# Two-layer kernel on one Trainium2 core: ranks counted with shifted keys, SSM step sizes of the first batch from TensorE, first tiles copied within SBUF, last outputs begun in two parts, and a new order of layer 1

## The reference, cut to what matters

```python
# L1_attn: a Mamba block; d_inner 512, 16 states
xz = x @ W_in.T; u, z = split(xz)
u = silu(causal_conv4(u) + b); dt, Bm, Cm = split(u @ W_x.T)      # dt: one value per token
delta = softplus(dt * W_dt + b_dt)                                # 512 channels
h_t = exp(delta_t * A) * h_(t-1) + delta_t * u_t * B_t            # 512 channels x 16 states
y = (sum_n h * C + D * u) * silu(z) @ W_out.T
# L1_ffn: light attention in windows of 128 (8 heads), plus heavy attention of 256 routed queries
scores = coor_descent(x . routing_token, k)                       # 50 iterations
sel = top_k(scores, 256)                                          # equal scores: the earlier token first
```

## Time and profile before

| what | value |
|---|---|
| three runs | 1880.72, 1887.73, 1896.94 us; median 1887.73 |
| the profiled execution | 1893.86 us, its span 1892.1 us |
| mean granted TensorE clock | 0.959 of full speed |
| busy over the span | PE 89%, DVE 81%, POOL 72%, ACT 71% |
| layer 1 starts | 633.2 us |
| first scan, end of the last product with C | 699.8 us, 1875.4 us |
| batch 0: end of du 0.0, scan 2, end of `ranks`, scan 18 | 678.5, 703.9, 731.8, 749.5 us |

### The profile page before, as it was taken

One profiled execution on the slowest core, in us unless ns is written; L12 is line 12 of the kernel. 1 busy time (PEld: TensorE's weight loads), 2 busy tenths in 40 slices (PEclk: granted clock), 3 DMA queues, 4 the chain that ended last, 5 costly groups with the idle time before them and its releaser, 6 DMA issues. The chain is left out here.

```text
span 1892.1 us, 44180 instructions
## 1 busy us (share of the span) xinstructions
PE 1687.4 (89%) x13508; PEld 1025.8 (54%) x13508; DVE 1540.8 (81%) x2806; ACT 1337.3 (71%) x3257; POOL 1354.6 (72%) x1115
## 2 busy tenths in 40 slices
PE   6899899799697568879999999989999999999987
PEld 4576576576475234335556546545545645644645
DVE  6547657556437789999999999999989999999997
ACT  4566566465364486776887896897797798787775
POOL 2706615806806228879899899889889889988996
PEclk9899899799798889989999999999999999999999
DMA  9346345445436563435236435346436346454430
GB/s 293 100 130 139 109 125 125 138 141 128 119 101 160 163 179 105 132 122 143 81 127 168 119 94 168 101 114 168 123 114 167 102 130 159 105 143 133 118 89 24
DMA packets 160088, 245.77 MB, mean 130 GB/s; under 512 B 30672, under 2 KB 105040, under 8 KB 159856
## 3 DMA queue, kind: packets, MB, share of 16 engines
q1 hardware_dynamic: 147568, 226.15, 42.3%
q0 software_dynamic: 12288, 16.79, 4.3%
HBM read 169.39 MB, written 73.47 MB: 128 GB/s over the span
## 5 line engine op out<-in xcount | busy, mean ns | idle before, releaser
L2254 POOL TENSOR_TENSOR HB<-DD,BC 128x512 f32<-128x512 f32 x512 | 643.4, 1285 | 110.5 <-DMA DD<-dd_scratch 55.1
L2581 ACT ACTIVATE bank<-DD,A 128x512 f32<-128x512 f32 x512 | 349.9, 696 | 138.1 <-DVE HB L2792 89.1
L2260 POOL TENSOR_TENSOR HB<-HB,BC 128x512 f32<-128x512 f32 x256 | 323.5, 1279 | 61.1 <-DVE HB L2787 58.4
L2787 DVE TENSOR_TENSOR_SCAN bank<-bank,HB 128x512 f32<-128x512 f32 x256 | 310.7, 1214 | 16.6 <-ACT bank L2581 15.1
L2787 DVE TENSOR_TENSOR_SCAN HB<-bank,HB 128x512 f32<-128x512 f32 x256 | 310.0, 1211 | 17.0 <-ACT bank L2581 14.5
L2792 DVE TENSOR_TENSOR HB<-bank,BC 128x512 f32<-128x512 f32 x256 | 174.8, 683 | 14.5 <-DVE bank L2787 0.5
L692 POOL DMA_INDIRECT X<-expert_out_scratch,slot x64 | 112.2, 1752 | 67.3 <-DMA expert_out_scratch<-YS 39.5
L2303 PE MATMUL bank<-HB,fold 128*32 128x512 f32 x1024 | 138.6, 613 | 22.9 <-DVE HB L2792 9.5
L2393 PE MATMUL bank<-ident,PR 128*128 128x128 f32 x768 | 115.3, 283 | 27.6 <-ACT PR L2619 18.8
L2303 PE MATMUL bank<-XRT,Wk 128*128 128x512 f32 x256 | 126.0, 625 | 11.2 <-ACT Qa L2595 8.6
L2393 PEld LDWEIGHTS bank<-ident,PR 128*128 128x128 f32 x768 | 86.5, 143 | 89.0 <-issue 40.0
(11 more groups left out here) (289 smaller groups left out, 3756.8 us busy)
## 6 DMA issues: line engine op xcount, KB each, us to landing
DD<-dd_scratch SPq DMA_DIRECT2D x512, 128.0 KB, 3.4
ROW<-row_scratch SPq DMA_DIRECT2D x64, 256.0 KB
BC<-ssm_scratch SPq DMA_DIRECT2D x128, 128.0 KB, 4.2
US<-us_scratch SPq DMA_DIRECT2D x32, 512.0 KB, 4.6
XL<-sorted_scratch SPq DMA_DIRECT2D x92, 128.0 KB, 2.1
expert_out_scratch<-YS SPq DMA_DIRECT2D x92, 128.0 KB, 1.8
us_scratch<-U SPq DMA_DIRECT2D x8, 1024.0 KB, 5.5
us_scratch<-SD SPq DMA_DIRECT2D x7, 1024.0 KB, 7.6
```

Of the source, the lines that this page charges most:

```text
L2254: done(pool.tensor_tensor(HB[:, c % HR], du, bc, ALU.mult), "dbu")
L2260: done(pool.tensor_tensor(h, h, bc, ALU.mult), "cg")
L2581: done(act.activation(PD[n % 2][:], delta, ACT.Exp, scale=A[:, k:k + 1]), "dA")
L2787: done(dve.tensor_tensor_scan(h if n % 2 else dA, dA, h, 0.0, ALU.mult, ALU.add), "scan")
```

## The change

1. **Ties.** `before` and L2774 go. The keys are also stored to a scratch `keypad` (a row of 256 per tile: 128 entries of -1, then the tile's 128 keys). A new step `w_ld` of each batch reads for partition p the 128 values that end just before token p's own key: KW, in the second half of Sel. The ties are then the count of equal values, a `tensor_scalar` with accumulation on KW alone. `ranks` becomes one `tensor_reduce` over 128 x 4 x 3. `w_ld` waits on SP for `del` b.1 (and the earlier readers of Sel), and each `rank` waits on DVE for the window to land. The first half of `keypad` is filled by one DMA from a memset.
2. **dt of batch 0.** A new step `dtb` on PE: four matmuls with column 0 of W_x broadcast to 128 columns put dt on all partitions of a bank; `abs` and `relu` of batch 0 read it there. `dt_ld` 0 goes. `ssm` 0 stays, for B and C, and stands behind `dtb` on PE.
3. **First tiles.** DD tiles 0 to 5 of batch 0 no longer come from `dd_scratch`: SP copies them from SD and U in SBUF, 8 DMAs of 32 x 512 per tile, after `del` 0.0 and `du` 0.0. `dd_st` of batch 0 is one step for all 512 channels; it waits for `del`, `du` 0.1 and for these copies to have landed.
4. **Tables.** The table with exp and ln is loaded just ahead of the first step that needs it after a silu. `gsilu` 0 moves up behind `silu`.
5. **Last outputs.** In batch 7, `tail` is split: `tailp` does the selection part and gates 0 to 2 of a tile's output, `tail` only the last matmul.
6. **Order.** All of `L1_ORDER` is written anew.

The diff, cut to its core (the order table is left out):

```diff
-    return [(kind, b, i)] if kind in ("in", "xt", "st") or kind in COPIES.values() else []
+    if kind == "tailp" or (kind == "tail" and b == B - 1):
+        return [("tail", b, i)] if kind == "tailp" else []
+    return [(kind, b, i)] if kind in ("in", "xt", "st", "dtb") or kind in COPIES.values() else []
...
+        KW = KJ[:, 1].rearrange("p (t j) -> p t j", t=NT)
...
+                def w_ld(b):
+                    sp.wait_ge(over["key_out"], 48)
+                    sp.wait_ge(over["pad_out"], 16)
+                    after(sp, "del", b, 1)
+                    after(sp, "xg", b - 1, 0)
+                    after(sp, "st", b - 1, 0, 1)
+                    earlier = scr["keypad"][b * NT:(b + 1) * NT]
+                    window = bass.AP(earlier.tensor, earlier.offset, [[1, P], [2 * P, NT], [1, P]])
+                    sp.dma_start(KW, window).then_inc(over["window_in"], 16)
...
-                def first_dd_st():
+                def first_dd_ld(i):
+                    after(sp, "del", 0, 0)
                     after(sp, "du", 0, 0)
-                    for c, src in enumerate((SD, U)):
-                        sp.dma_start(scr["dd"][0, 0:2 * P, c].rearrange("(k p) t -> p k t", p=P), src[:, pair(0)]) \
-                          .then_inc(over["first_dma"], 16)
+                    k, rows = i // 4, slice(32 * (i % 4), 32 * (i % 4) + 32)
+                    for st in range(4):
+                        for c, src in enumerate((SD, U)):
+                            sp.dma_start(DD[32 * st:32 * st + 32, i, c], src[rows, k]).then_inc(over[f"dd_in{i}"], 16)
...
                 def dd_st(b):
+                    after(sp, "del", b, 0, 1)
                     after(sp, "du", b, 0, 1)
+                    if b == 0:
+                        for i in range(DDS):
+                            sp.wait_ge(over[f"dd_in{i}"], 128)
...
+                def first_steps():
+                    loaded(pe, 0, "small_in")
+                    bank = claimed(pe, "dtb", 0, 0)
+                    for k in range(NB):
+                        after(pe, "silu", 0, k)
+                        q = mm(bank[:], Wx[:, k, 0:1].broadcast_to([P, P]), U[:, k], k == 0, k == NB - 1)
+                    done(q, "dtb")
...
+                for what, b, i in plan:
+                    if what in SILUS1:
+                        with_exp = False
+                    elif what in EXPS1 and not with_exp:
+                        load_ln_exp(act)
+                        with_exp = True
...
                 def rank(b, t):
...
                     dve.wait_ge(over["key_in"], 32 * (b + 1))
+                    dve.wait_ge(over["window_in"], 16 * (b + 1))
...
-                    own(dve.scalar_tensor_tensor(out=KJ[:, 1, 0:P], in0=KR[:, own_tile], scalar=KC[:, t:t + 1],
-                                                 in1=before[:], op0=ALU.is_equal, op1=ALU.mult,
-                                                 accum_out=ties[:, t:t + 1]))
+                    own(dve.tensor_scalar(KW[:, t], KW[:, t], KC[:, t:t + 1], None, ALU.is_equal, ALU.add,
+                                          accum_out=ahead[:, t, 2:3]))
...
-                    own.now(dve.tensor_tensor(ties[:], ties[:], ahead[:, 1], ALU.add))
-                    done(dve.tensor_tensor(ties[:], ties[:], ahead[:, 0], ALU.add), "ranks")
+                    done(dve.tensor_reduce(ties[:], ahead[:], X_AXIS, ALU.add), "ranks")
```

More of the change, by code:

```diff
@@ new lines @@
+    "gsilu": [[73]],
+    "us_st": [[76, 184], [506], [1129], [1818], [2368], [3113], [3660], [4312]],
+    "dtb": [[77]],
+    "abs": [[78, 79, 81, 82], [605, 571, 572, 607], [1181, 1170, 1171, 1182], [1852, 1819, 1820, 1853], [2439, 2431,
+        2438, 2455], [3117, 3115, 3116, 3122], [3776, 3722, 3723, 3777], [4372, 4371, 4380, 4373]],
+    "sexp": [[80, 102], [635], [1205], [1868], [2498], [3139], [3791], [4409]],
+    "ssm": [[87], [531], [1136], [1766], [2392], [3041], [3683], [4305]],
+    "ssmc": [[88], [532], [1137], [1767], [2393], [3042], [3692], [4309]],
@@ L1897, in pairs_of @@
     return sorted({m // 2 for m in items_of(a)})
+SILUS1, EXPS1 = {"silu", "gsilu"}, {"es", "asc", "sexp", "sln", "dA", "expl", "exp"}
 COPIES = {"xrtc": "xrt", "zc": "z", "ssmc": "ssm", "projc": "proj", "xgc": "xg", "turnc": "turn", "tailc": "tail", "spreadc": "spread"}
@@ L1922, in bank_freed @@
         return "pv", b, i if kind == "widenc" else NT + i
+    if kind == "relu" and b == 0:
+        return ("dtb", 0, 0) if i == NB - 1 else None
     if kind in HALVES:
@@ L2192, in _ @@
                         k_ld(b)
+                    elif what == "w_ld":
+                        w_ld(b)
                     elif what == "x_ld":
@@ L2238, in constants @@
                     own(pool.memset(half[:], -0.5))
[L2239 to L2243 removed]
+                    own(pool.memset(pad, -1.0))
+                    own.now(pool.memset(fold[:], 0.0))
                     for r in range(4):
@@ L2443, in fold_states, with tail_begun @@
                     done(q, "fold")
-                def tail(b, t):
-                    after(pe, "gate", b, *range(NB))
+                def tail_begun(b, t):
                     after(pe, "widenr", b, 0, 1)
@@ L2463, in _ @@
                         scan_in(what, b, i)
+                    elif what == "dtb":
+                        first_steps()
                     elif what == "ssm":
@@ L2483, in _ @@
                         fold_states(b, i)
+                    elif what == "tailp":
+                        tail_begun(b, i)
                     elif what == "tail":
@@ L2623, in widened_reciprocals @@
                     after(act, "rec", b, a)
+                    if b == 0 and a == 0:
+                        act.wait_ge(over["pad_out"], 16)
                     if a:
```

300 lines of the change are left out of this document (150 added, 150 removed), and 505 rows, old and new, of the table L1_ORDER.

## The result

The changed kernel takes 1879.9 us (median of 20 runs), beside 1888.6 us for the kernel before: a ratio of 0.9944, 95% interval [0.9925, 0.9962]. It is faster, by 0.56% by the ratio (the medians lie 8.6 us apart), where 1.4% or 27 us was forecast. The profiled execution took 1881.7 us, span 1880.0.

What follows compares the result with a forecast made beforehand. DVE and PE were taken to share the bound at 94% in layer 1's long stretch. Terms -20 + 2 - 6 - 3 = -27 took 1893.9 to 1866.9, scaled to 1861 us; range 1838 to 1884.

Steps and rivals of the forecast that it cites:

- Ties and ranks: DVE's tie counts and rank additions in layer 1: 42.7 us of DVE freed, of which 20 us shorten the kernel.
- The rival in which all of it shows: Long stretch of layer 1: a new order uses all 42.7 us of DVE freed, giving 1838 us; 14%.
- the rival in which PE takes DVE's place: Long stretch of layer 1: PE bounds, the ties give only 4.3 us, so 1877 us; 24%.
- That the count doesn't do what it says: Rival on DVE's tie counts: the one-tensor count in place still stands behind POOL, giving 1881 us; 5%.
- The wait for the window: DVE ahead of each batch's first `rank`: waiting for the window load costs 2 us, mostly in batch 7.
- The start: Start of layer 1, batch 0: new orders, copies of first tiles and fewer table loads save 6 us.
- copies at over 1 us of issue: Sign of being wrong, on SP's queue at the start: each copy within SBUF takes over 1 us to issue.
- The last rival: SP's queue at the start: 48 copies choke it, at 1.5 us each giving 1912 us; 7%.
- The other signs of being wrong: DVE idle before a batch's first `rank`, POOL awaiting DD tiles beyond 705, PE's share still 94% with DVE's down.
- The end: Last batch's outputs after the last gate: matmuls begun early save 3 us; moving `widen` ahead costs nothing.
- At nothing: `dtb` on PE, `kst`'s third DMA, the filling of `keypad` and `dd_st` 0 as one step: costed at 0 us.
- The rule on `tensor_reduce`: DVE's new reductions: a `tensor_reduce` never contends with GpSimd, so 2.7 us holds for the eight.

Runs made afterwards that it cites:

- e3_old_ties: The changed kernel with the old count of ties on two tensors and its two additions, without the window load: 1914.5 us, ratio 1.0103 to the kernel before.
- e2_ties_alone: The kernel before with only the new count of ties, its one reduction and the window load: 1882.5 us, ratio 0.9966.
- e7_double_copies: The changed kernel with each of the 48 copies of the first six tiles cut into two of half the bytes: 1906.8 us, ratio 1.0097.
- e1_scratch: The changed kernel with batch 0's first tiles stored to scratch and loaded from it, as before: 1865.2 us, ratio 0.9867; 0.9897 when run again.
- the filler: Two unread DVE maxima put ahead of each new tie count: ratio 1.0136 when added to `e1_scratch`, 1.0072 when added to `e2_ties_alone`.
- e9_scratch_keys: `e1_scratch` with the loads of tiles 4 and 5 of batch 0 moved behind those of keys and window: 1863.2 us, ratio 0.9891.

## Why the prediction was right and wrong

**1. Ties and ranks (-20).** The durations were right: counts at 343 ns, the reduction at 165 ns, which makes 1.3 us in all where 2.7 were taken, and 44.0 us freed for 42.7. The effect of steps 1 and 2 and of the new order together is the -14.4 us of the middle, where -18 was said: 3.6 off. That it came so near is luck, for the reason was wrong. "Half, since DVE and PE bound alike" is the mean of two things that don't mix: in the new order all of it counts (-31 to -36), in the old one on balance an eighth (the 8.4 and the -4.8 of its stretches 1 and 4 nearly cancel), and the order costs 17 to 22 of it. The rival in which all of it shows is what the new order does with DVE's time; the old one gives a gain as small as the rival in which PE takes DVE's place. The forecast left out that a new order has a price of its own. Why it has one isn't settled: no run moves single steps of it. That the count doesn't do what it says is out, by the 343 ns. And the additions were blocked, as the forecast took them to be: 887 and 678 ns on average in the kernel before, 280 and 292 in `e3_old_ties`.

**2. The wait for the window (+2).** DVE stands twice as long as taken, and the place was wrong. Behind 740 it stands 4.2 us in all in front of a `rank`, where it didn't stand before: 1.7 in batch 1, 1.3 in batch 2 and 1.2 in batch 3. The last two end as `KR` lands; the keys' loads stand behind the window's in SP's queue. For the first the profile names no releaser:

```profile
828.92 0.38 SPq L2108 DMA_DIRECT2D Sel<-keypad_scratch  x1
833.53 0.75 DVE L2824 TENSOR_SCALAR_CACHE_REDUCE Sel<-KR,KC 128x512 f32<-128x512 f32 x1 [1.74 <-issue]
```

The keys had landed long before, and the trace has this window land at 833.4, 4.5 us after its issue (3.2 to 5.4 over the batches): it was the window, issued as late as `del` 1.1 allowed. `e2_ties_alone` has the same wait, 3.3 us, with the window named. Batch 7, where the forecast looked for it, had none.

**3. The start (-6).** This is the step that failed: "8 DMAs per tile at 0.42 us of issue". The 0.42 was that of a load from DRAM; a copy within SBUF takes 0.63. 48 x 0.21 = 10 us more of SP. Layer 1 begins 2.8 us sooner in this trace, so the forecast's times have to be counted from the layer's begin (633.4 before, 630.6 here):

| from the layer's begin | before | forecast | measured |
|---|---|---|---|
| end of du 0.0 | 45.2 | 46.5 | 48.5 |
| first tile at POOL | 54.1 | 52.6 | 56.2 |
| scan 0 | 66.4 | 64.4 | 66.8 |
| third tile at POOL | 61.1 | 68.1 | 75.8 |
| scan 2 | 70.5 | 69.3 | 77.2 |

Some 2 us were lost before the first copy. `del` 0.0 was to wait for DVE's own passes and no longer for ACT; it still waited 2.1 us for ACT, which had itself stood 2.0 us for weights:

```profile
668.31 0.72 ACT L2547 ACTIVATE Wv<-Wv,gamma 128x512 f32<-128x512 f32 x1 [2.04 <-DMA Wv<-in_L_ffn_wkv_heavy]
675.34 1.23 DVE L2899 TENSOR_TENSOR SD<-XT,SD 128x1024 f32<-128x1024 f32 x1 [2.12 <-ACT XT L2617]
```

Then the slower issue holds up the third tile by 5.7 us more than forecast. Behind it comes what the step had not worked out at all: `kst` and the key loads behind the copies, 7.3 us of DVE. In place of -6 the start gave +6.5. With the scratch way it gave -7.3 and -1.4 in two runs: the rest of the step (early keys, tables, order) was sized well or somewhat too high. There were two table loads between 650 and 720, as said.
The warning sign "copies at over 1 us of issue" was set by the total; the true one was lower, since the forecast's own chain let every us of SP pass to scan 2. The last rival had mechanism and place right, and only the size wrong: 0.63, where it asked for 0.98 to turn the sign. `e7_double_copies`, with 1.26 us for what was one copy, is slower than before by 1%, as it should be by that rule. The other signs of being wrong did show: POOL waits for a tile until 706.4, and DVE stands in front of the first `rank` in four batches.

**4. The end (-3).** Measured -1.4, and for another reason. "Moving `widen` ahead costs nothing" was true and probably not enough: 1.7 us come without the early beginning. The early beginning itself, sized at 3.2, gives nothing that lasts (17.3 us from scan 511 to the end, 17.1 without it): PE is at the folds up to 1865.8, and only 0.65 us of the new early matmuls (from 1866.76) got ahead of the gate's end at 1867.41.

**5. At nothing.** `dtb` and the filling of `keypad` stayed hidden; `kst` didn't, for the reason under 3, and `ranks` 0 ended 100.8 us after the layer's begin, not 89.3. `dd_st` 0 cost nothing: scan 18 stands 120.5 us after the beginning, 8.4 later than before, all of which scan 8 (12.2 later) already had.

**Sum.** Forecast -6 (start), -18 (ties, window and order) and -3 (end); measured +6.5, -14.4 and -1.4. Of the 17.7 us between -27 and -9.3, 12.5 are the start. Without the copies the change gives 22 us (0.9882, the mean of the two ratios of `e1_scratch`), near the 27 said. PE's clock was no part of the difference: 0.99 in the long stretch before, 1.00 after.

The rule on `tensor_reduce` that the prediction drew on held: the Trainium skill, "SBUF — State Buffer", section "Who interferes with whom". Four of the eight reductions ran while POOL was busy and all took 156 to 167 ns; of the filler's 64 maxima 52 did, and all took 673 to 687. The same page of the Trainium skill says, in "Summary: rules for kernel authors", that of a DVE instruction with two SBUF inputs and a GpSimd one that reads SBUF the second to issue blocks until the first finishes. The trace goes further: the count of 10.52 us wasn't let in between eight products.

## What to carry to other kernels

Measure what an engine's time is worth before you spend effort on it: put as much idle work as you mean to take away into the same places and look at the length. Here some 37 us of it cost 44 us in one order and 19 in the other by the ratios (36 to 42 and 7 in the traces). An edit and the order of work made for it are one change: here the order alone was a loss, and the edit alone gave 6 us. And price a DMA by its issue on the queue that issues it, with the number for its own kind of source, then list all that stands behind it in that queue.

The best version here is `e1_scratch` (or `e9_scratch_keys`): the change with its first tiles by way of scratch, ratio 0.987 to 0.990 to the kernel before, where the change has 0.994.

## Not expected

- A copy of 32 partitions within SBUF takes 0.63 us from issue to issue, with 2 KB or 1 KB per partition alike; a load from DRAM with twice the bytes of the larger 0.43.
- DMAs whose source is a broadcast with 4 as its first dimension kept the DMA engines 0.18 to 0.26 busy, and one behind another each stood 4.2 us at its issue; four DMAs of 32 partitions, the same bytes, took 0.43 us each, with all engines busy (1.04).
- Layer 0 took some 57 us less on one chip than on the others, layer 1 nearly the same (1236.7 and 1241.8 us for the same kernel). Ratios to a kernel timed on the same chip hold; times from different chips don't compare.
